# Rebuilding the preparation of a four-layer vision kernel: index spread by TensorE, biases as a weight row, later weights made inside layer 1

## The reference

```
x = x + _L0_conv_ref(_gn(x), qkv_w, qkv_b, proj_w, proj_b, rpb_table, rel_index)   # window attention, 12 heads of 8
x = x + _L1_conv_ref(_gn(x), w_qkv, w_out, b_out, pos_emb)                         # shifted windows, 12 heads of 32
x = x + _L2_conv_ref(_gn(x), w_dw, w_pw)                                           # 3x3 depthwise + 1x1, ternary weights
x = x + _L3_conv_ref(_gn(x), q_w, ..., p_var)                                      # spiking attention, batch norms
```

## Time and profile before

| what | value |
|---|---|
| time, median of 3 runs (lowest to highest) | 438.77 us (437.97 to 439.72) |
| time of the profiled execution, its span | 439.99 us, 438.1 us |
| PE busy, DVE busy, ACT busy, POOL busy | 87%, 73%, 56%, 45% of the span |
| first norm of layer 0 on ACT | starts at 46.99 us |
| first bias addition of layer 0 on DVE | starts at 54.97 us |

### The profile page before, as it was taken

The page is one execution under the profiler, slowest core; times in us unless marked ns, Lnnn a source line. Parts: engine busy times, 40 slices in busy tenths (PEclk is TensorE's granted clock), DMA queues, the critical chain, the costliest instruction groups (busy, mean ns, idle before and its releaser), DMA issues.

```text
span 438.1 us, 13521 instructions
## 1 busy us (share of the span) xinstructions
PE 382.5 (87%) x4971; PEld 282.5 (64%) x4971; DVE 320.0 (73%) x730; ACT 246.3 (56%) x554; POOL 197.1 (45%) x319
## 2 busy tenths in 40 slices
PE   0178599999999999999999999999999999858773
PEld 0168377888888787777777777777777533325441
DVE  0488288777787867878777777777878679965783
ACT  0010366878778675665666666666566455457871
POOL 8202056675666754445444444444544352442341
PEclk9999999999999999999999999999999999997996
DMA  8900000000000000000000000000000000000111
GB/s 290 166 9 1 0 4 1 4 0 0 0 0 0 3 2 3 2 1 1 2 3 1 0 0 0 0 0 1 1 2 3 1 0 0 1 0 18 39 37 54
DMA packets 8520, 7.15 MB, mean 16 GB/s; under 512 B 5058, under 2 KB 8130, under 8 KB 8354
## 3 DMA queue, kind: packets, MB, share of 16 engines
q1 hardware_dynamic: 3984, 5.26, 4.1%
q10 hardware_dynamic: 4498, 1.38, 1.8%
HBM read 5.06 MB, written 1.57 MB: 15 GB/s over the span
## 4 chain that ended last, share of the span: by engine, by line
PE 63%; DVE 16%; issue 9%; POOL 4%; DMA 3%; ACT 3%; DVEq 0%; POOLq 0%; ACTq 0%
PE bank L726 12%; PE bank L760 12%; PE bank L789 11%; PE bank L769 9%; PE bank L736 6%; DVE conv L1238 5%; PE bank L833 4%; PE bank L818 3%; DMA table<-in_L_conv_rpb_table 3%; POOL y_out L1437 2%; PE bank L555 2%; DVE stats L584 2%; DVE row_max L961 2%; PE bank L835 1%; PE bank L1346 1%
## 5 line engine op out<-in xcount | busy, mean ns | idle before, releaser
L999 POOL TENSOR_TENSOR probs<-probs,row_max 128x384 f32<-128x384 f32 x128 | 105.5, 830 | 128.4 <-DVE row_max L961 127.7
L957 DVE TENSOR_TENSOR probs<-bank,bias 128x384 f32<-128x384 f32 x128 | 65.4, 552 | 56.6 <-PE bank L760 56.4
L860 ACT ACTIVATE probsT<-bank 128x384 f32<-128x384 f32 x128 | 61.2, 492 | 63.7 <-PE bank L769 63.7
L961 DVE TENSOR_REDUCE row_max<-probs 128x6 f32<-128x384 f32 x128 | 68.2, 545 | 1.0
L769 PE MATMUL bank<-cst,probs 128*128 128x128 f32 x384 | 62.6, 280 | 0.0
L760 PE MATMUL bank<-k,q 64*64 64x128 f32 x1536 | 58.0, 282 | 3.7 <-ACT k L907 1.9
L789 PE MATMUL bank<-v,probsT 128*64 128x18 f32 (+1 forms) x1536 | 57.7, 219 | 1.2 <-DVE headsN L986 0.8
L760 PEld LDWEIGHTS bank<-k,q 64*64 64x64 f32 x1536 | 42.4, 135 | 25.3 <-issue 24.3
L789 PEld LDWEIGHTS bank<-v,probsT 128*64 128x64 f32 x1536 | 50.1, 137 | 12.6 <-issue 11.7
L923 DVE COPY v<-bank 64x384 f32<-64x384 f32 (+1 forms) x96 | 46.8, 487 | 9.6 <-PE bank L736 7.2
L769 PEld LDWEIGHTS bank<-cst,probs 128*128 128x128 f32 x384 | 44.4, 140 | 10.9 <-issue 5.0
(11 more groups left out here) (137 smaller groups left out, 581.4 us busy)
## 6 DMA issues: line engine op xcount, KB each, us to landing
rel_bc<-in_L_conv_rel_index SPq DMA_DIRECT2D x1, 2048.0 KB, 8.8
x<-in_x SPq DMA_DIRECT2D x4, 384.0 KB, 12.2
out_dram<-y_out SPq DMA_DIRECT2D x8, 192.0 KB, 2.1
w<-in_L_conv_w_qkv ACTq DMA_DIRECT2D x1, 432.0 KB, 4.9
cst<-in_consts ACTq DMA_DIRECT2D x1, 421.0 KB
p<-in_L_conv_w_out ACTq DMA_DIRECT2D x1, 144.0 KB, 4.7
pos<-in_L_conv_pos_emb SPq DMA_DIRECT2D x8, 2.0 KB
b_qk<-in_L_conv_qkv_b ACTq DMA_DIRECT2D x8, 0.1 KB, 6.8
```

Of the source, the lines that this page charges most:

```text
L860: nc.scalar.activation(probsT[w][:, :], ps_probsT[w % 2][:, 0:NP * 128], ACT.Exp).then_inc(L.s.probsT_sb, 1)
L957: nc.vector.tensor_tensor(out, scores, b, ALU.add).then_inc(L.s.biased, 1)
L961: nc.vector.tensor_reduce(row_max[w][:, :], probs[w][:, :, :], AX.X, ALU.max).then_inc(L.s.maxed, 1)
L999: nc.gpsimd.tensor_tensor(probs[w][:, :, :], probs[w][:, :, :], by_row(row_max[w]), ALU.subtract).then_inc(L.s.shifted, 1)
```

## The change

1. The index matrix is loaded as 8 rows of 512 (16 KB), turned to bf16 by DVE, and spread over 128 partitions by 8 matmuls of 128x512; ACT copies each from PSUM (`rel_all`). DVE compares in 4 pieces of 1024 columns, with the statistics of x between them.
2. The bias is gathered for keys k and k + 32 in turn, on partitions 0 to 63 and 64 to 127 of a bank (3 banks of 14 keys). DVE sums into `bias_half`; two copies on DVE and two on ACT lay out `bias0`.
3. The q, k, v biases of layer 0 are row 97 of the weights; row 97 of `xn` is one. The evacuations have no bias.
4. The table is split on POOL. The zeroing is in two parts; the later part comes after the first norm.
5. ACT issues 4 DMAs only; SP issues all the others, late loads last. `cst` is loaded in two parts.
6. `pos` and the turned projection weight come after the first scores (`pe_pos`, `dve_pos`).
7. The weights of layers 2 and 3 are made by jobs `"w3"`, `"pw"`, `"bn"`, `"pwT"` in calls B, B + 1, B + 3 and 2B - 3 of `*_sample` (B = 16; call B works on the first sample of layer 1).

```
@@ sp_loads
+            sp.dma_start(rel_rows, a["L0_conv_rel_index"].rearrange("(i q) k -> i (q k)", i=REL_ROWS)).then_inc(rel_in, 16)
+            sp.dma_start(cst[:, 0:N_FIRST], a["consts"][:, 0:N_FIRST]).then_inc(const_in, 16)
...
@@ dve_prepare
+            compare(0)
+            first_stats(0)
+            compare(1)
+            first_stats(1)
+            compare(2)
+            dve_norm_in(dve, 0, 0)
+            compare(3)
+            done["onehot"] = count[0]
+            dve_norm_out(dve, 0, 0)
+            first_stats(2)
+            first_stats(3)
...
@@ act_prepare
+            act.wait_ge(zeroed, ZEROED)
+            nc.scalar.activation(act_first_exp[:, :], w0T[:, 0:1], ACT.Exp).then_inc(first_exp, 1)
+            for i in range(REL_ROWS):
+                act.wait_ge(rel_spread, i + 1)
+                nc.scalar.copy(rel_all[:, i * REL_COLS:(i + 1) * REL_COLS], bank[i % 3][:, :]).then_inc(rel_copied, 1)
...
@@ pe_bias
+                    for t, n in ((0, REL_LO), (1, REL - REL_LO)):
+                        for h in range(2):
+                            sel = onehot[0:n, t, :].rearrange("r (q k) -> r q k", k=WT)[:, :, k + h * 32]
+                            last = nc.tensor.matmul(bank[2 + i][h * WT:(h + 1) * WT, (k - k0_) * 3 * HEADS:(k - k0_ + 1) * 3 * HEADS],
+                                                    sel, table_parts[0:n, t, :, :], start=(t == 0), stop=(t == 1))
...
@@ dve_weights_out, job "bn" (five steps of 96x384, four of 96x4)
+                step(nc.vector.tensor_copy(w3_parts[0:C, 0, :], w3))
+                step(nc.vector.tensor_tensor(w3_rest[:, 0, :], w3, w3_parts[0:C, 0, :], ALU.subtract))
...
@@ pe_sample
+            if norm and nxt2:
+                pe_qkv(pe, *nxt2, 1, 2)
             if norm:
-                pe_qkv(pe, *nxt2, 1, 2)
-                pe.wait_ge(gn_step, gn_count(*norm) * STEPS)
+                if norm in done:
+                    pe.wait_ge(dve_prep, done[norm])
+                elif norm in NORMS:
+                    pe.wait_ge(gn_step, gn_count(*norm) * STEPS)
...
@@ pe_first
+            pe_bias(pe, 0, 1)
             pe_qkv(pe, L0, 0, 0, 2)
+            pe_bias(pe, 1, 3)
             pe_scores(pe, L0, 0, 0)
             pe_qkv(pe, L0, 0, 2, 3)
             pe_qkv(pe, L0, 1, 0, 2)
+            pe_pos(pe)
```

More of the change, by code:

```diff
@@ L561, in pe_late_weights, with compare @@
-        def pe_late_weights(pe):
-            pe.wait_ge(dve_prep, done["pw_abs"])
-            for j in range(4):
-                last = nc.tensor.transpose(bank[1][0:C, (1 + j) * C:(2 + j) * C], w3_raw[:, j, :], ident[0:C, 0:C])
-            last.then_inc(pe_prep, 1)
-            nc.tensor.matmul(bank[0][0:C, 0:1], ones[0:C, 0:C], pw_abs[:, :], start=True, stop=True).then_inc(pe_prep, 1)
+            def compare(i):
+                cols = slice(2 * i * REL_COLS, 2 * (i + 1) * REL_COLS)
+                dve.wait_ge(rel_copied, 2 * i + 2)
+                for t in range(2):
+                    step(nc.vector.tensor_scalar(onehot[:, t, cols], rel_all[:, cols], cst[0:REL_LO, lo + t:lo + t + 1], None,
+                                                 ALU.is_equal))
@@ new lines, in pe_pos, with columns @@
+        def pe_pos(pe):
+            pe.wait_ge(pos_in, 16 * WIN)
+            pe.wait_ge(p0_in, P0_IN)
+            for j in range(2):
+                both = const("perm", WT)[:, j * 128:(j + 1) * 128]
+                for xb in range(j + 1):
+                    def columns(ap, b):
+                        return ap if j == 0 else ap.rearrange("q (y b x) -> q y b x", b=2, x=4)[:, :, b, :]
+                    nc.tensor.matmul(columns(ps_mix[:, j * WT:(j + 1) * WT], xb), both, columns(pos[:, :], xb ^ 1),
+                                     start=True, stop=True)
+            nc.tensor.transpose(ps_mix[0:C, 2 * WT:2 * WT + C], p0_raw[:, :], ident[0:C, 0:C]).then_inc(mix_ready, 1)
@@ new lines, in dve_pos, with pe_weights @@
+        def dve_pos(dve):
+            dve.wait_ge(mix_ready, 1)
+            dve.wait_ge(p0_in, P0_IN)
+            prep(nc.vector.tensor_tensor(bias1[:, :, :], ps_mix[:, 0:2 * WT].rearrange("p (j k) -> p j k", j=2),
+                                         const("masks").rearrange("p (j k) -> p j k", j=2), ALU.add))
+            prep(nc.vector.tensor_copy(p0T[0:C, :], ps_mix[0:C, 2 * WT:2 * WT + C]))
+            done["pos"] = count[0]
+        def pe_weights(pe, what):
+            if what == "w3":
+                pe.wait_ge(late_in, LATE_IN)
+                for j in range(4):
+                    last = nc.tensor.transpose(ps_mix[0:C, j * C:(j + 1) * C], w3_raw[:, j, :], ident[0:C, 0:C])
+            elif what == "pw":
+                pe.wait_ge(dve_prep, done["pw_abs"])
+                last = nc.tensor.matmul(ps_mix[0:C, 0:1], ones[0:C, 0:C], pw_abs[:, :], start=True, stop=True)
+            elif what == "pwT":
+                pe.wait_ge(dve_prep, done["pw_u"])
+                last = nc.tensor.transpose(ps_mix[0:C, 0:C], pw_u[:, :], ident[0:C, 0:C])
+            last.then_inc(weights_ready, 1)
@@ L1528, in _ @@
             pe_prepare(pe)
-            pe.wait_ge(dve_prep, done["all"])
             pe_first(pe)
@@ L1538, in _ @@
         def _(act):
-            act.wait_ge(table_in, TABLE_IN)
-            nc.scalar.activation(act_first_exp[:, :], cst[:, 0:1], ACT.Exp).then_inc(first_exp, 1)
-            act.wait_ge(dve_prep, done["all"])
-            act.wait_ge(late_in, LATE_IN)
+            act_prepare(act)
             act_first(act)
```

455 lines of the change are left out of this document (254 added, 201 removed).

## The result

The changed kernel takes 418.88 us (median of 4 runs, 417.52 to 419.33); the kernel before, run in turn with it, 438.58. The ratio is 0.953, with a 95% interval of 0.950 to 0.956. Two further sets of runs, each beside the kernel before, gave 416.60 (after_again; ratio 0.947, 0.944 to 0.951) and 416.87 (after_third; 0.948, 0.946 to 0.951). The forecast was 414.6, its own range 410 to 418, the whole range 409 to 423. The kernel is faster as forecast, and the forecast was too low by 4.3 us in the first set, which lies outside its own range and inside the whole one, and by 2.0 and 2.3 in the later ones.

A forecast was written before the change was run, and what follows sets the result against it. Preparation up to the first bias addition was taken to bound the kernel, PE the layers behind. 27.7 us earlier, less 1.0 for pos and 2.5 for weight jobs, gave 24.2 less: median 414.6, own range 410 to 418, whole 409 to 423.

The forecast's parts named there:

- What bounds it: Preparation is worth nearly its full length up to the first bias addition; behind it only what is added on PE.
- Steps (a) to (c): Start up to the whole one-hot: POOL's zeroing to 5.3, ACT's copies to 10.3, DVE's compares and statistics to 15.5.
- lower bound: DVE's compares with both operands bf16: twice the rate, 0.39 a compare, 2.1 less in all.
- Step (d): PE's 56 bias matmuls of bank 0 at 0.056 by alternating halves, done at 18.6, the same as POOL's arm.
- Rival 1: Column halves don't overlap: 128 bias matmuls at 0.114 instead of 0.056, 7.4 more, 422.0; chance 0.20.
- Step (e): Products 1.20, 72 bias matmuls 4.0, then scores, v copies: first addition at 27.3, 27.7 us earlier.
- (c): DVE as the chain from 6.8: compares at 0.65 each, statistics, norm steps; the one-hot whole at 15.5.
- Step (f): `pe_pos` before the next scores and `dve_pos` before the next additions give 1.0 back.
- Layer 1 and 2: Weight jobs cost w3 1.1, pw 0.5, bn 0 (hidden), pwT 0.9: sum 2.5, between 1.3 and 5.
- Sum: 27.7 - 1.0 - 2.5 = 24.2 us less: span 413.9, profiled execution 415.8, median 414.6.
- Rival 2: The start hangs elsewhere: x lands late (statistics 3.4 later) or POOL's late fills run 1.6 late; about 418, chance 0.13.
- Rival 3: PE's low clock, entered in its pause from about 10 to 15.5, holds over layer 0: 462, slower; chance 0.02.

The follow-up runs named there:

- after_again: The changed kernel itself, unedited, run again beside the kernel before: 416.60 us, ratio 0.947.
- after_third: The changed kernel itself, unedited, run once more as control beside the kernel before: 416.87 us, ratio 0.948.
- index_broadcast: Changed kernel with the index loaded as a 2 MB int32 broadcast again, no spread by PE or copies by ACT: 424.26 us, ratio 0.966.
- halves_apart: Changed kernel with the same 128 bias matmuls ordered one column half after the other in each bank, not alternating: 423.65 us, ratio 0.965.
- warm_start: Changed kernel plus seven f32 matmuls nothing reads, four ahead of the index spread and three ahead of the first norm matmul: 416.83 us, ratio 0.949.
- pos_early: Changed kernel with the pos matmuls and their steps moved from between the two additions to ahead of the first norm matmul: 416.58 us, ratio 0.947.
- jobs_on_pool: Changed kernel with eleven DVE steps of the weight jobs (five of bn, six of pw) moved to POOL in the same calls: 416.06 us.

## Why the prediction was right, and where it was off

**What bounds it** held. The first addition came 27.5 us earlier by the mechanism forecast, and what the layers gave back is what PE and DVE got to do on top, and the clock. Undone one at a time, the spread of the index, the alternation and the move of the weight jobs put the first addition back by 5.4, 5.2 and 7.8 us, 18.4 together. The other 9.1 (the table split on POOL, the zeroing, the order of the loads, `pos`, the early norm) was not taken apart.

**Steps (a) to (c)** came out close: their end came 1.0 earlier than forecast. ACT's first exponential stood at 5.66 (forecast 5.3), the copies took 0.50 each and ended at 9.75 (10.3). A compare of 1024 columns took 0.50 instead of the 0.65 assumed, so the one-hot was whole at 14.5 and not 15.5. The lower bound was 0.39, from twice the rate of the int32 row. The instructions alone take 0.486 with bf16 input, and with int32 input 0.752 for 1024 columns (index_broadcast) and 2.352 for 4096. The last two give 0.52 ns a column and a fixed part of 0.22 us. If bf16 has the same fixed part, an assumption, it is at 0.26 ns a column: twice the rate, diluted by the fixed part to a factor of 1.5 on the whole instruction. So the lower bound had the rate right and the fixed part at about half. The Trainium skill's "VectorE: DVE Perf Modes" (section "Mode 4×_2P — both tricks at once") has the faster mode for this form, and on this reckoning the runs agree.

**Step (d)** held: 56 bias matmuls in 3.27 (forecast 3.1), 0.058 each (0.056). **Rival 1** is refuted by halves_apart, 0.096 to 0.105 on one half. By the rule of the Trainium skill's "TensorE: Matmul & The Clock Gate" (section "The mechanism"), that loads overlap only where the row group differs, the alternation should have brought nothing. Here only the column half differs, and the saving is there; that it is the load that overlaps is the forecast's reading, which the runs support and do not separate from matmuls of the two halves running side by side.

**Step (e)** had an error that took back the gain of (c). Bank 0 was done at 17.87 and the norm at 17.84 (18.6 each in the forecast), but the products were put at 1.20 us, a row of two records. An f32 matmul of this width has two records in these traces (the four added in warm_start have eight), so the two products ahead of the second burst are four, 2.07 us: the row was the part of a group that lay on the chain, not the whole group. The first addition came at 27.45 for 27.3, so two errors, 0.7 too late and 0.9 too short, cancelled: that this step came out to 0.15 is luck.

**Step (f)** is the first mis-sized term: 1.0 was forecast between the first addition and the norm job of the second call, 2.2 measured in the first profile, 0.0 in after_again (27.5 lead at both places). By itself pos costs 0.6 there (pos_early against the control), where the forecast had 1.0. The rest is the moment of the clock's rise, which the forecast did not have as a term: it took the earlier trace rows's 1.00 at the start as the upper level, and the first clock record of that trace is at 58.2. I also read the durations of the earlier trace rows, 0.114 for a bias matmul, as if at the same level as the 0.034 of the earlier trace rows. The halving survived, because both of its orders run at the lower level.

**Layer 1 and 2** is the second mis-sized term and the surer one: 4.24 for 2.5, repeated in every profile of the changed kernel. w3 and pw cost 2.15 (forecast 1.6), bn 0.82 (0), pwT 1.27 (0.9). The step that failed is the one for bn: it looked for cover at the next scores, where PE comes late enough, and not at the wait behind them, the head copy of the next round, to which DVE carries its delay. DVE is busy 75% of the span, but between two rounds it has gaps of 1.0 to 1.5 only, and what does not fit there is carried on. jobs_on_pool shows it from the other side: the steps off DVE, the waits gone, 1.7 back, 0.8 of it in bn's stretch.

**Sum.** 413.9 + 0.15 (first addition) + 1.2 (f) + 1.7 (jobs) = 416.95, and 416.8 was measured; with the early rise 413.9 + 0.15 - 1.0 + 1.7 = 414.75, and 414.6 was measured. The time outside the span was 2.5 in the first profile and 1.8 in after_again, and the forecast took over the 1.9 of the kernel before; it also took over that the profiled execution lies 1.2 above the median, where it lay 0.5 above it in the first set and 0.2 below it in after_again.

**Rival 2** did not come: x landed 7.3 us after its issue (median of its four loads) and not 12.2, the first statistics started at 7.98, and POOL ended its late fills at 26.35 with 2.73 us to wait before its first subtraction. That its price of about 418 lies nearest to the first median is a coincidence:

```profile
x<-in_x SPq DMA_DIRECT2D x4, 384.0 KB, 7.3
...
25.54 0.81 POOL L410 MEMSET v<- 64x24 f32 x4
29.08 1.61 POOL L1103 TENSOR_TENSOR probs<-probs,row_max 128x384 f32<-128x384 f32 x2 [2.73 <-DVE row_max L1065]
```

**Rival 3**, the low clock, was there, in both kernels and smaller by far than priced: in the changed kernel not entered in the pause but never left before 28 to 36 us. The text argued against it with the clock column, and that argument was unsound, as the column shows 1.00 before its first record. Here the rule of the Trainium skill's "TensorE: Matmul & The Clock Gate" (section "What's actually happening") that the low level is the idle engine's default was the better guide, and the column the worse.

## What to carry to other kernels

Price PE's work at the start of a kernel by durations from its own start, not by the steady ones and not by the clock column: the same 24 matmuls took 1.56 and 0.89 us here. When a job is put on an engine with small gaps, follow its delay to the next place where the bounding engine waits for that engine, not only to the next instruction; 0.8 us here came from steps that looked hidden. Fit a short instruction's time from two lengths, a fixed part and a rate, before scaling it. And take a second profile of the same program before explaining 2 us: of the 2.2 that pos seemed to cost, the control left 0.6.

## What was not expected of the hardware

The moment at which TensorE's durations fall to those of the upper level moved between 28 and 36 us for one program, and moved the end by 2.2 us. The two bias bursts with the products between them, 9.4 us of unbroken PE work of which 7.4 in thin bf16 tiles, passed at the lower level. In warm_start the clock rose at 4.15 us, fell back at 7.57 and then stayed at 0.50 for 20 us, in which PE was busy for 17.9; with two more f32 matmuls ahead the upper level was there at 14.1 us. And small loads issued beside a broadcast load of 2 MB land late: the bias of layer 0 (1.1 KB) at 17.8 us and the table at 15.3, where the bias is there by 8.9 and the table by 7.1 in the changed kernel.
